# Attention and mixture of experts on one core: attend and the next scores side by side, value units together, output product behind the first key unit

## The reference

```
x = x + attention(layernorm(x), ctx, ctx)      # 16 heads of 64, causal, softmax(q k^T / 8) v, then @ Wo + bo
u = layernorm(x);  z = layernorm(u) * g + b
w = the two largest of softmax(z @ rW + rb), of 8 experts, normalised to sum 1
x = x + u + sum_e w_e (gelu(z @ W1[e] + b1[e]) @ W2[e] + b2[e])
```

## Time and profile before

| | before |
|---|---|
| median of 3 runs | 1026.72 us (1025.11 to 1026.84) |
| span of the profiled execution, first to last instruction | 909.4 us |
| device time of the profiled execution itself | not listed; median less span is 117.3 us |
| mean granted TensorE clock | 0.977 |
| busy TensorE, VectorE, ScalarE, GpSimd | 843.1, 742.4, 607.9, 501.6 us |
| the regular attention groups | 41.25 us each |

### The profile page before, as it was taken

How to read it: one execution, slowest core, us unless ns; L and a number is a source line. 1 busy time by engine, 2 the same in 40 slices (tenths; PEclk the granted TensorE clock), 3 DMA queues, 4 the chain that set the end, 5 groups by cost and what they waited for, 6 DMA issues and landing times. The chain is left out here.

```text
span 909.4 us, 35805 instructions
## 1 busy us (share of the span) xinstructions
PE 843.1 (93%) x13368; PEld 741.3 (82%) x13368; DVE 742.4 (82%) x2243; ACT 607.9 (67%) x1317; POOL 501.6 (55%) x605
## 2 busy tenths in 40 slices
PE   9999899999999999999999999999988979997860
PEld 6888798988889888988889988988877867776750
DVE  5896779898989888898989998999776886666864
ACT  5677666777667776677767776676846744555753
POOL 3732545363746455354646455354446777777771
PEclk9999999999999999999999999999989999999995
DMA  9200101010110101010100101000103343336756
GB/s 289 60 25 3 41 12 41 6 41 9 41 34 15 35 12 41 6 41 6 41 24 29 35 12 38 9 29 6 44 14 86 101 136 107 106 106 180 241 176 219
DMA packets 55670, 56.72 MB, mean 62 GB/s; under 512 B 7335, under 2 KB 48593, under 8 KB 55601
## 3 DMA queue, kind: packets, MB, share of 16 engines
q1 hardware_dynamic: 46651, 37.94, 14.5%
q0 software_dynamic: 8640, 17.84, 5.8%
q10 hardware_dynamic: 310, 0.08, 0.0%
HBM read 32.62 MB, written 23.23 MB: 61 GB/s over the span
## 5 line engine op out<-in xcount | busy, mean ns | idle before, releaser
L901 PE MATMUL bank<-in_h,Ah 128*128 128x256 f32 x654 | 207.4, 317 | 15.1 <-DVE Al L1566 14.7
L771 ACT ACTIVATE pr<-pr 128x512 f32<-128x512 f32 x128 | 80.8, 631 | 184.4 <-DVE pr L1270 184.4
L700 POOL DMA_INDIRECT mixed<-kf,ix_i x142 | 141.1, 994 | 48.6 <-issue 38.9
L724 ACT ACTIVATE kf<-bank 128x512 f32<-128x512 f32 x256 | 157.3, 615 | 2.8 <-PE bank L905 1.9
L905 PE MATMUL bank<-in_h,Al 128*128 128x256 f32 x512 | 144.5, 282 | 0.0
L902 PE MATMUL bank<-in_l,Ah 128*128 128x256 f32 x512 | 144.3, 282 | 0.0
L605 POOL DMA_INDIRECT slots<-zrow,slot_ix x120 | 122.7, 1023 | 36.8 <-issue 22.7
L901 PEld LDWEIGHTS bank<-in_h,Ah 128*128 128x128 f32 x654 | 124.5, 190 | 22.7 <-DVE Al L1566 19.0
L1016 PE MATMUL bank<-wo_s,oT 128*128 128x128 f32 x1024 | 133.9, 285 | 0.9 <-ACT oT L766 0.9
L1280 DVE TENSOR_TENSOR pr<-pr,ri 128x512 f32<-128x512 f32 x128 | 130.1, 1016 | 4.4
L540 POOL TENSOR_TENSOR idle_p<-half 128x1 f32<-128x1 f32 x121 | 41.1, 342 | 167.3 <-DVE slot_ix L1361 144.9
(11 more groups left out here) (192 smaller groups left out, 1915.3 us busy)
## 6 DMA issues: line engine op xcount, KB each, us to landing
kf<-slots SPq DMA_DIRECT2D x71, 130.0 KB
kf<-mixed SPq DMA_DIRECT2D x12, 512.0 KB, 5.0
xs<-in_x_dram SPq DMA_DIRECT2D x16, 256.0 KB, 3.2
c_in<-in_ctx_dram SPq DMA_DIRECT2D x16, 256.0 KB, 3.0
out_dram<-xs SPq DMA_DIRECT2D x16, 256.0 KB
mixed<-kf,ix_i POOLq DMA_INDIRECT x142
vf<-mixed SPq DMA_DIRECT2D x4, 512.0 KB, 4.9
slots<-zrow,slot_ix POOLq DMA_INDIRECT x120
```

The costliest lines, as they stand in the source:

```text
L700: pool.indirect_dma_start(out=mixed, out_offset=bass.IndirectOffsetOnAxis(ap=ix_i[buf][:, j:j + 1], axis=0), in_=y_sb[buf][:, j, :], in_of ...
L724: act.activation(kfs[par][:, 2 * u:2 * u + 2, :], ring[gr.bank(name)].rearrange("p (h t) -> p h t", h=2), ACT.Copy).then_inc(act_ev, 1)
L901: pe.matmul(ps, lh, rh, start=True, stop=False)
```

## The change

Four things move; no arithmetic changes. The first value unit leaves the head of the pair and stands directly ahead of the second. The input unit leaves the head of pairs 0 and 2 and stands between the second value unit and attend of the pair before (P2 in pair 1; in pair 3 it is named P4 and belongs to the next group; a first P4 is done before group 0). Attend is then followed directly by the scores of the next pair; their mask wait moves before the last matmul of the second value unit (products_ready). The output product goes behind the first key unit. The logits stand between the two value units. ScalarE follows the same order, GpSimd's scatters and prep and SyncE's load are released by other units. VectorE's order stays as it was.

```diff
@@ pair_units, orders @@
-    p = [f"P{i}"] if i % 2 == 0 else []
+    p = [f"P{i + 1}"] if i % 2 == 1 else []
-    return p + [v[0], k[0], t[0], k[1], t[1]] + routing + [k[2], k[3], v[1]] + o + (["RL"] if i == 2 else [])
+    return [k[0], t[0], k[1], t[1]] + routing + [k[2], k[3], v[0]] + (["RL"] if i == 2 else []) + [v[1]] + p + o
-ORDER_START = ["P2"] + [f"K{i}{a}" for i in (2, 3) for a in range(4)]
+ORDER_START = ["P2"] + [f"K{i}{a}" for i in (2, 3) for a in range(4)] + ["P4"]
@@ SyncE @@
-            def load_next(gr, g, last=False):
-                sp.wait_ge(unit, gr.done("P0"))
+            def load_next(kept, g, last=False):
+                sp.wait_ge(unit, kept.done("P4"))
@@ GpSimd @@
-                send_at(g - 2, gr, "P0", 2)
-                prep(g + 1, gr.done("P0"), between=lambda: send_at(g - 2, gr, "V00", 3),
-                     ahead=lambda: send_at(g - 2, gr, "T00", 4))
+                send_at(g - 2, gr, "K00", 2)
+                prep(g + 1, group_of(g - 1).done("P4"), between=lambda: send_at(g - 2, gr, "T00", 3),
+                     ahead=lambda: send_at(g - 2, gr, "K01", 4))
                 send_at(g - 2, gr, "O00", 5)
                 x1_centre(g - 1)
-                send_at(g - 2, gr, "V10", 6)
+                send_at(g - 2, gr, "K10", 6)
@@ ScalarE, group @@
-                    if i % 2 == 0 and not (last and i == 2):
-                        input_unit(gr, f"P{i}", 1 - i // 2)
-                    exp_half(n, par, 0)
-                    value_unit(gr, f"V{i}0", n, par)
                     if keyed:
                         key_unit(gr, f"K{i}0")
-                    exp_half(n, par, 1)
+                    exp_half(n, par, 0)
                     if not (first and i == 0):
                         t_unit(gr, f"T{i}0", n - 1, 0)
+                    exp_half(n, par, 1)
...
-                    value_unit(gr, f"V{i}1", n, par)
+                    for k in range(2):
+                        value_unit(gr, f"V{i}{k}", n, par)
+                    if i % 2 == 1 and not last:
+                        input_unit(gr, f"P{i + 1}", i // 2)
@@ TensorE @@
+            def products_ready(gr, n, i, attends, ends):
+                if attends:
+                    heads_free(gr, i)
+                if not ends:
+                    scores_ready(n + 1, (i + 1) % GP, gr)
@@ TensorE, group @@
-                    if f"P{i}" in gr.order:
-                        input_unit(gr, f"P{i}", g + i // 2, 1 - i // 2)
                     if first and i == 0:
-                        pe.wait_ge(pro_l, 5)
-                    value_unit(gr, f"V{i}0", i, lambda: scores_ready(n, i, gr if i else kept))
+                        scores_ready(n, i, kept)
                     scores(n, i)
+                    if keyed:
+                        if i % 2 == 0:
+                            pe.wait_ge(dve_ev, gr.done("P2", 1) if i else kept.done("P4", 1))
+                        key_unit(gr, f"K{i}0")
                     if not (first and i < 2):
                         project(n - 2, gr.done(f"O{i - 1}1", 0) if i else kept.done("O31", 0))
-                    if keyed:
-                        if i % 2 == 0:
-                            pe.wait_ge(dve_ev, gr.done(f"P{i}", 1))
-                        key_unit(gr, f"K{i}0")
...
-                    value_unit(gr, f"V{i}1", i, (lambda: heads_free(gr, i)) if attends else None)
+                    value_unit(gr, f"V{i}0", i)
+                    if i == 2 and not first:
+                        r_logits(gr)
+                    value_unit(gr, f"V{i}1", i, lambda: products_ready(gr, n, i, attends, last and i == GP - 1))
+                    if i % 2 == 1 and not last:
+                        input_unit(gr, f"P{i + 1}", g + 1, i // 2)
                     if attends:
                         attend(gr, i, 1 - par)
-                    if i == 2 and not first:
-                        r_logits(gr)
@@ VectorE, group @@
-                    if f"P{i}" in gr.order:
-                        input_unit(gr, f"P{i}", 1 - i // 2)
+                    if i == 0:
+                        input_unit(start if first else kept, "P4", 1)
+                    if i == 2 and not last:
+                        input_unit(gr, "P2", 0)
```

More of the change, by code:

```diff
@@ L418, in load_next @@
                                  x_t[:, bass.ds(g * GP + 2 * GP, GP), :]).then_inc(ld_x, 16)
[L420 to L423, removed]
+            load_next(start, 0)
+            load_next(group_of(0, True), 1)
+            with aligned_loop(mybir.EngineType.SP, 2, NG - 2) as g:
+                load_next(group_of(g - 1), g)
+            load_next(group_of(NG - 3), NG - 2, last=True)
             def pad():
@@ L638, in _ @@
             prep(0)
-            prep(1, group_of(0, True).done("P0"))
+            prep(1, start.done("P4"))
             split_w1()
-            prep(2, group_of(1).done("P0"))
+            prep(2, group_of(0, True).done("P4"))
             x1_centre(0, first=True)
@@ L646, in _ @@
             send_at(0, group_of(1), "O31", 1)
-            send_at(0, group_of(2), "P0", 2)
-            prep(3, group_of(2).done("P0"), between=lambda: send_at(0, group_of(2), "V00", 3),
-                 ahead=lambda: send_at(0, group_of(2), "T00", 4))
+            send_at(0, group_of(2), "K00", 2)
+            prep(3, group_of(1).done("P4"), between=lambda: send_at(0, group_of(2), "T00", 3),
+                 ahead=lambda: send_at(0, group_of(2), "K01", 4))
             send_at(0, group_of(2), "O00", 5)
             x1_centre(1)
-            send_at(0, group_of(2), "V10", 6)
+            send_at(0, group_of(2), "K10", 6)
             send_at(0, group_of(2), "T11", 7)
@@ L671, in _ @@
             send_at(NG - 3, group_of(NG - 2), "O31", 1)
-            for q, name in enumerate(("P0", "V00", "T00", "O00")):
+            for q, name in enumerate(("K00", "T00", "K01", "O00")):
                 send_at(NG - 3, end, name, q + 2)
             x1_centre(NG - 2)
-            send_at(NG - 3, end, "V10", 6)
+            send_at(NG - 3, end, "K10", 6)
             send_at(NG - 3, end, "T11", 7)
@@ L826, in _ @@
                         seed(0, hf)
+            input_unit(start, "P4", 1)
             group(0, first=True)
@@ L1101, in group @@
                     attends = not (first and i == 0)
-                    value_unit(gr, f"V{i}1", i, (lambda: heads_free(gr, i)) if attends else None)
+                    if first and i == 0:
+                        pe.wait_ge(pro_l, 5)
+                    value_unit(gr, f"V{i}0", i)
[4 more added lines that the diff above has]
+                        input_unit(gr, f"P{i + 1}", g + 1, i // 2)
                     if attends:
@@ L1118, in _ @@
                 key_unit(start, f"K3{k}")
+            input_unit(start, "P4", 0, 1)
             group(0, first=True)
```

## The result

| kernel | where | median us | ratio to the kernel before, 95% interval |
|---|---|---|---|
| before | upper level, 11 runs | 1029.34 | |
| changed | upper level, 11 runs | 1038.17 | 1.0093 [1.0072, 1.0114] |
| changed, again | upper level | 1035.57 | 1.0102 [1.0070, 1.0134] |
| before | lower level | 910.86 | |
| changed (after_fourth) | lower level | 930.57 | 1.0229 [1.0192, 1.0265] |

The times of one kernel fall into two levels from session to session, 910 and 1027 us for the kernel before, on a chip with the same number too; every ratio here is between runs of one session, and differences in us between runs of two sessions are rough by some 1 us. The profile from which the prediction was made is of the lower level, the first timed runs are of the upper.

What follows compares the result with a forecast made beforehand. TensorE was taken to set the pace; after the move, waits for VectorE's in_l add 13 x 1.64 = +21.3 us, less 3.7 from other pairs: +17.6, span 927.0, 1044 us; range 1012 to 1055.

Steps and rivals of the forecast that it cites:

- in_l's cover: First key units of pairs 0 and 2 wait for VectorE's in_l, 1.2 and 1.0 us; +0.67 and +0.97 us a group.
- The sum: Whole kernel: +21.3 us from 13 regular groups, -3.7 from 12 other pairs, +17.6 us in all.
- The 12 pairs at the ends: Pairs in the first two groups and the last, without that VectorE load, gain 0.31 us each: -3.7 us.
- 117 us lie around the span: Median 1026.72 us against a profiled span of 909.4: 117.3 us taken to lie around the span, unchanged.
- ScalarE's wait: Before the second value unit's last matmul: 0.55 us in pair 1, 0.28 in pair 3; free unless in_l is in time.
- TensorE's own 40.0: TensorE alone, without waits of this kind, would go through a group in about 40.0 us.
- rival 1: TensorE stays the bound, in_l in time: 1008 us, or 1020 with ScalarE's waits of 0.83 a group; chance 0.24.
- The junction: Attend directly ahead of scores: attend costs 0.96 us, nothing extra for the passage, bounds 0 to 0.13.
- The logits: Between pair 2's value units: 0.18 us more; routing chain over 1.3 us behind pair 3's scores' start, its 1.78 wait gone.
- GpSimd: Scatters and prep move to later units, prep some 2 us later; effect on stretched VectorE normalise products taken as 0.
- The clock: TensorE would wait 2.2 of 42.9 us a group; no fall of its granted clock taken.
- My own sign of being wrong: TensorE idle below 0.5 us a group in the regular groups, or a gap from attend to scores.

Runs made afterwards that it cites:

- after_fourth: The changed kernel, unchanged, run again at the lower level against the kernel before; 930.57 us, ratio 1.0229.
- inl_first: The changed kernel with in_l ahead of statistics and masks (pair 0) and of the routing's second part (pair 2) on VectorE; 924.69 us, ratio 1.0157 to the kernel before.
- before_fifth: The kernel before, unchanged, run again at the upper level; 1026.62 us.
- before_fourth: The kernel before, unchanged, run again at the lower level; 910.51 us.

## Why the prediction was right, and where it was not

**in_l's cover: right in place, and in what it adds to a group.** K00 starts 323.18 - 310.42 = 12.76 us behind S3 (12.74 forecast), K20 343.83 - 331.46 = 12.37 behind S1 (12.24). The chains, VectorE's from S1 and from the rank products, set them as worked out. A group grew by 42.70 - 41.14 = 1.56 us (1.64 forecast). TensorE's wait itself was forecast at 1.2 us in K00 and 1.0 in K20; the rows have 0.93 and only 0.40 (0.04 in K20 of the last three groups). TensorE came later to K20 than forecast (S1 to S2 took 10.74 where I had 10.2), by ScalarE's wait and by longer scores, both below. Since VectorE's chain sets when K20 starts, what TensorE loses on the way there changes the wait and not the sum.

**The sum: right at the level it was made from, in part by luck.** 930.57 - 910.86 = 19.7 us against 17.6; at the upper level 8.8, where other costs enter (below). The 13 regular groups gave 13 x 1.56 = 20.3 (21.3 forecast). The 12 pairs at the ends, which were to give back 3.7, gave back nothing: the last scores start at 691.1 against 670.3 us, 20.7 later. The expert phase, taken as untouched, was 2.1 us shorter (237.2 against 239.2); traces of the kernel before differ by 2.5 among themselves there. My reading that 117 us lie around the span was wrong. That the absolute forecast of 1044 us lies near the 1038.17 measured at the upper level is luck: it is a sum made at the lower level, put on a base of the upper.

**ScalarE's wait: right in kind, mis-sized.** The last value matmul of pair 1 started at 340.36, where TensorE's pieces give 332.78 + 0.80 + 1.79 + 3.03 + 0.70 + 0.47 = 339.57: 0.79 and not 0.55. Ahead of pair 0 it is 0.51 and not 0.28. ScalarE's copies there:

```profile
336.00 0.60 ACT L753 ACTIVATE pT<-bank 128x512 f32<-128x512 f32 x1 [1.06 <-PE bank L986]
...
339.49 0.62 ACT L725 ACTIVATE kf<-bank 128x512 f32<-128x512 f32 x1
```

K13's copy starts 8.03 behind S1 (7.83 forecast), since T0's is 4.54 behind it (4.35). It ends at 340.11, and the matmul starts 0.25 later, which I had at nothing; ahead of pair 0 it is 0.25 too. TensorE in turn was 0.21 later than my 7.90, which gives the 0.24 between 0.55 and 0.79. "They cost nothing here" held for the changed kernel. But "were in_l in time, they would cost 0.83 a group" failed: inl_first's group of 42.08 is 2.1 above TensorE's own 40.0. With that, rival 1's time of 1020, that is 6 us below before, failed as well; such a kernel is 15 us above it. The term mis-sized is the wait before the last value matmul, 0.83 for the key copies and 0.1 for the seeds in my text. In inl_first it is 1.99 us a group from start to start: 1.41 ahead of pairs 0 and 2, where I had the 0.83, and 0.58 ahead of pairs 1 and 3, where I had 0.1 or nothing. TensorE's 40.0 and these 1.99 make up the 42.08 to within 0.1.

**The junction: right.** 0.98 us against 0.96; nothing extra. The Trainium skill, "TensorEngine Tiling (Array Packing)", section Key Properties, says that a change of the tiling mode drains the array. The trace agrees: attend takes 0.98 us up to scores, where the mode stays, and took 1.09 up to the value unit, where it changed. What I did not see is that scores of pair 1 now take 332.78 - 331.46 = 1.32 us up to the key unit, those of pair 3 1.04; those of pair 2 can't be read here, for the wait for in_l follows them. Why they take longer is open.

**The logits: nearly.** The routing chain was over 311.73 - 310.42 = 1.31 us behind S3 (1.3 forecast), the wait for rank products is 1.37 (1.2), 0.28 of the logits' wait stayed.

**GpSimd: right.** The stretched products of pair 0 are 1.36 and 2.03 us; the latter is in the rows above, 2.22 before.

**The clock: right at the lower level, wrong at the upper.** There attend of pair 1 breaks into pieces in every group, and in three of the eleven groups scores and key unit behind it run at half clock. My own sign of being wrong, a gap from attend to scores, did not come at the junction, but 0.4 us inside attend three times. TensorE of one of the three groups in order of time, then the granted clock (the column behind POOL's):

```profile
309.20 1.14 PE L1003 MATMUL bank<-pT,vf 64*64 64x64 f32 x45
...
310.76 0.39 PE L1003 MATMUL bank<-pT,vf 64*64 64x64 f32 x6 [0.42 <-issue]
...
311.56 0.33 PE L1003 MATMUL bank<-pT,vf 64*64 64x64 f32 x3 [0.41 <-issue]
...
312.27 0.50 PE L1003 MATMUL bank<-pT,vf 64*64 64x64 f32 x10 [0.38 <-issue]
...
312.47 2.01 PE L1041 MATMUL bank<-kf 64*64 64x64 f32 x64
...
314.41 0.58 PE L903 MATMUL bank<-in_h,Ah 128*128 128x256 f32 x1
```

```profile
309.00:312.00 3.00, 2.06 (x57) 1.46 (x56) 2.32 (x12) 0.96 (x2) 2.35 (x4) 1.00 0.07 22
312.00:313.00 1.00, 0.72 (x30) 0.71 (x32) 0.00 (x0) 0.23 (x1) 0.00 (x0) 0.73 0.20 67
313.00:316.00 3.00, 3.00 (x63) 2.88 (x58) 1.45 (x3) 0.86 (x2) 2.38 (x4) 0.52 0.00 0
```

The clock was 0.52 of full, the lower level of 1.2 GHz, from 313 to 316 us, behind 3 us of which TensorE was busy 2.06. Scores took 1.94 us and the key unit 1.45 where 1.04 and 0.80 are usual. It does not fall behind such pieces each time: one group earlier TensorE was busy 2.02 of 3 us with the same pieces (263.6 to 266.6 us of the same run), and the clock stayed at 1.00.

**Why the loss is smaller at the upper level.** A group of the kernel before is 45.23 - 41.14 = 4.09 us longer at the upper level, in all four pairs (1.44, 0.65, 1.64, 0.35); 2.1 of it are idle time in the trace, the rest lies inside the pieces. A group of the changed kernel is 3.06 longer, made up of three things. S1 to S2, with attend in pieces, is 3.07 longer in every group. S2 to S3 is 10.49 to 10.54 us in eight of the eleven groups, up to 0.5 shorter than at the lower level (11.05, in the last three groups 10.63): scores start so late that nothing is left of the wait for in_l in K20. In the other three it is 12.0 to 12.1, by the fallen clock. That these two cancel in the mean is chance. S3 to S0 and S0 to S1 are those of the lower level to 0.01; there attend and scores show no gap in the trace, and the wait for in_l in K00 is 0.9 us as before. Why they run whole there is not shown.

## What to carry to other kernels

When a step is moved up on one engine, look at what it had in front of it: the piece removed from between an operand's producer and its use was the cover, and slack has to be read there, not at the engine's busy share. Take out two such waits together before judging an order, since each alone hides behind the other: 6 and 8 us became 24.6. Look at single groups before you read a mean: at the upper level two unlike effects cancelled in it. And take a profile's own time from a run of the same session before building a sum on it.

## What the runs showed of the hardware

At the upper level runs of small matmuls (a weight load and a matmul every 0.015 us) break off, in the rows above after 43 to 46 of 64, with 0.37 to 0.49 us between the pieces, at nearly the same places of each group; at the lower level the same lists run whole. Together the attention phase of the kernel before is 53 us longer (the last scores start at 722.9 against 670.3) and the expert phase 65 us (304.1 against 239.2); of the changed kernel 40 and 64. In the expert phase the mean granted clock of the kernel before is 0.81 in before_fifth and 0.93 in before_fourth, and TensorE is busy for 217 and 183 us and idle for 87 and 57; whether the lower clock or the idle time comes first is not shown. The lower clock can't explain the attention phase, where the regular groups of the kernel before have 1.00 in both. DMAs move the same bytes (56.72 MB). Instructions that come late would look like this, but what makes a session slow was not found, and no run here tells.
